# An adaptive-norm attention and feed-forward layer: three late query products instead of two, and their copies behind each step's exponential

## What is computed

```
x = x + attn(cond(x, cond_128, ...), Wq, Wkv, Wo, bo)
x = x + ffn(cond2(x, cond_128, ...), w1, w3, w2, lora...)
attn: q = x@Wq (32 heads of 16), k, v = x@Wkv (8 groups of 16)
      weights = softmax(where(causal, -inf, q k^T) * 0.25);  ctx = weights v;  out = ctx@Wo + bo
ffn:  h1 = lora_linear(x, w1), h3 = lora_linear(x, w3);  lora_linear(silu(h1) * h3, w2)
```

## Time and profile before

| | |
|---|---|
| time, median of 3 runs | 592.26 us (591.83 to 592.91) |
| time of the profiled execution | 592.54 us |
| span of the profiled execution | 590.7 us |
| mean granted clock of PE | 0.991 |
| busy: PE, DVE, ACT, POOL | 578.9, 237.6, 172.2, 182.3 us |
| chain, attention's part | first scores at 101.87 us, first context at 118.30 us; last POOL piece in it at 172.99 us |

### The profile page before, as it was taken

How to read it: one execution, slowest core, us unless ns; L and a number is a source line. 1 busy time by engine, 2 the same in 40 slices (tenths; PEclk the granted TensorE clock), 3 DMA queues, 4 the chain that set the end, 5 groups by cost and what they waited for, 6 DMA issues and landing times.

```text
span 590.7 us, 8111 instructions
## 1 busy us (share of the span) xinstructions
PE 578.9 (98%) x3227; PEld 466.8 (79%) x3227; DVE 237.6 (40%) x340; ACT 172.2 (29%) x296; POOL 182.3 (31%) x132
## 2 busy tenths in 40 slices
PE   9999999799999999999999999999999999999997
PEld 6988988577777778887778888778888777888885
DVE  1434542789999851111641111244111234211112
ACT  3561224564654353332121111121111102211110
POOL 3438463699999595434200000000000000000000
PEclk9999999969999999999999999999999999999999
DMA  7975648545666774000019000007400002200001
GB/s 244 344 306 158 225 161 267 144 102 172 178 157 178 240 220 88 1 0 1 1 71 226 5 1 1 2 1 206 94 0 0 0 0 76 67 0 1 0 1 71
DMA packets 70735, 59.24 MB, mean 100 GB/s; under 512 B 45072, under 2 KB 61840, under 8 KB 69584
## 3 DMA queue, kind: packets, MB, share of 16 engines
q1 hardware_dynamic: 69840, 57.43, 32.2%
q10 hardware_dynamic: 864, 1.38, 0.6%
HBM read 40.94 MB, written 16.79 MB: 98 GB/s over the span
## 4 chain that ended last, share of the span: by engine, by line
PE 84%; POOL 6%; DVE 4%; ACT 2%; SPq 1%; DMA 1%; issue 1%; POOLq 0%; DVEq 0%
PE twin L1333 41%; PE twin L1354 20%; PE twin L1155 7%; POOL probs L646 4%; PE twin L1299 3%; PE twin L1175 3%; PE twin L1188 3%; PE twin L1230 3%; DVE total L997 2%; ACT probs L822 2%; DVE top L980 2%; SPq L463 1%; POOL probs L653 1%; PE twin L1118 1%; DMA down_sb<-in_down_factors 1%; PE twin L1285 1%
## 5 line engine op out<-in xcount | busy, mean ns | idle before, releaser
L1046 DVE TENSOR_TENSOR gate<-twin,gate 128x512 f32<-128x512 f32 (+1 forms) x44 | 30.4, 691 | 244.5 <-PE twin L1333 244.5
L1333 PE MATMUL twin<-c_hi,f_lo 128*128 128x512 f32 (+1 forms) x352 | 96.5, 397 | 0.0
L1333 PE MATMUL twin<-c_hi,f_hi 128*128 128x512 f32 (+1 forms) x352 | 95.4, 393 | 0.0
L1333 PE MATMUL twin<-c_lo,f_hi 128*128 128x512 f32 (+1 forms) x352 | 95.3, 393 | 0.0
L1333 PEld LDWEIGHTS twin<-c_hi,f_lo 128*128 128x128 f32 (+1 forms) x352 | 65.6, 187 | 16.1 <-POOL f_lo L682 0.4
L1333 PEld LDWEIGHTS twin<-c_hi,f_hi 128*128 128x128 f32 (+1 forms) x352 | 65.5, 186 | 15.6 <-issue 0.3
L1333 PEld LDWEIGHTS twin<-c_lo,f_hi 128*128 128x128 f32 (+1 forms) x352 | 65.5, 186 | 15.5
L868 ACT ACTIVATE gate<-twin 128x512 f32<-128x512 f32 (+1 forms) x44 | 26.3, 598 | 169.9 <-PE twin L1333 169.9
L1354 PE MATMUL twin<-f_lo,gate_hi 128*128 128x512 f32 (+1 forms) x176 | 68.6, 390 | 0.0
L871 ACT CAST gate_hi<-gate 128x512 fp32r<-128x512 f32 (+1 forms) x44 | 27.3, 622 | 126.6 <-DVE gate L1046 126.6
L1354 PE MATMUL twin<-f_hi_head,gate_hi 128*128 128x512 f32 x128 | 50.1, 392 | 0.0
(11 more groups left out here) (150 smaller groups left out, 813.8 us busy)
## 6 DMA issues: line engine op xcount, KB each, us to landing
f_sb<-in_f SPq DMA_DIRECT2D x2, 2752.0 KB, 20.1
x_dram<-resid_stage SPq DMA_DIRECT2D x16, 256.0 KB, 2.1
rows<-x_dram SPq DMA_DIRECT2D x16, 256.0 KB, 3.5
q_t<-q_dram SPq DMA_DIRECT2D x8, 512.0 KB, 5.5
x_dram<-rows SPq DMA_DIRECT2D x16, 256.0 KB, 3.3
rows<-x_dram SPq DMA_DIRECT2D x8, 512.0 KB, 4.5
out<-rows SPq DMA_DIRECT2D x12, 256.0 KB, 2.0
x_sb<-in_x SPq DMA_DIRECT2D x2, 1024.0 KB, 7.6
```

The lines of the kernel that those rows point to most:

```text
L1046: dve.tensor_tensor(gate[0:w, h % 2, :], up_bank[2 * (h % 2) + 1][0:w, :], gate[0:w, h % 2, :], ALU.mult).then_inc(gate_ready, 1)
L1333: mm = pe.matmul(bank[0:w, :], f[:, c, :], c_part[:, c, :], start=(n == 0 and c == 0), stop=(n == 2 and c == DC - 1))
```

## The change

`LATE_Q` becomes 3: in the last block q1, q2 and q3 come behind the first scores, q1 and q2 both at step 1 and q3 at step 2 (`LATE_STEPS`). ACT's late copies go from ahead of the exponential to behind it, in the same steps as the projections. All four pieces of `wo_hi` are made ahead of the copy of q0. The four border memsets go from ahead of POOL's loop to its step 5, behind the second multiplication there, together with the wait for `wo_lo`. The packing of the convolution's weights stays at step 2 (`PACK_AT`).

```diff
-LATE_Q = 2
+LATE_Q = 3
+LATE_STEPS = (1, 1, 2)
+PACK_AT = 2
@@ POOL
-            pool.wait_ge(wo_lo_split, REP)
-            for pair in (near_head, near_tail):
-                pool.memset(pair[:, :, :, 0:1], 0.0).then_inc(near_zeroed, 1)
-                pool.memset(pair[:, :, :, WIN - 1:WIN], 0.0).then_inc(near_zeroed, 1)
...
             for n in range(QUADS + OUT):
...
+                if n == SUM + TILES:
+
+                    pool.wait_ge(wo_lo_split, REP)
+                    for pair in (near_head, near_tail):
+                        pool.memset(pair[:, :, :, 0:1], 0.0).then_inc(near_zeroed, 1)
+                        pool.memset(pair[:, :, :, WIN - 1:WIN], 0.0).then_inc(near_zeroed, 1)
@@ ACT, last block of the front
+                    if blk == BLOCKS - 1:
+
+                        act.wait_ge(wo_loaded, 16)
+                        for part in range(REP):
+                            act.copy(wo_hi[:, part, :]...).then_inc(wo_hi_split, 1)
                     for j in range(REP - (LATE_Q if blk == BLOCKS - 1 else 0)):
                         copy_queries(blk, j)
...
-                        if blk == BLOCKS - 1:
-
-                            act.wait_ge(wo_loaded, 16)
-                            for part in range(j * REP // (REP - LATE_Q), (j + 1) * REP // (REP - LATE_Q)):
-                                act.copy(wo_hi[:, part, :]...).then_inc(wo_hi_split, 1)
@@ ACT, attention
-                if 1 <= n <= LATE_Q:
-                    copy_queries(BLOCKS - 1, REP - LATE_Q + n - 1)
...
                     act.activation(probs[:, n % PROBS], probs[:, n % PROBS], ACT.Exp, scale=SCALE)\
                         .then_inc(exp_ready, 1)
-                if n == LATE_Q:
+                for k, step in enumerate(LATE_STEPS):
+                    if n == step:
+                        copy_queries(BLOCKS - 1, REP - LATE_Q + k)
+                if n == PACK_AT:
@@ PE, attention
-                if 1 <= n <= LATE_Q:
-                    project(BLOCKS - 1, REP - LATE_Q + n)
-                if n == LATE_Q:
+                for k, step in enumerate(LATE_STEPS):
+                    if n == step:
+                        project(BLOCKS - 1, REP - LATE_Q + 1 + k)
+                if n == PACK_AT:
                     group_conv()
```

More of the change, by code:

```diff
@@ L770, in _ @@
                                 .then_inc(k_loaded[0], 16)
+                    if blk == BLOCKS - 1:
+                        act.wait_ge(wo_loaded, 16)
+                        for part in range(REP):
+                            act.copy(wo_hi[:, part, :].rearrange("p (h r w) -> p h r w", h=2, r=BT),
+                                     in_windows(wo_sb[:, part, :])).then_inc(wo_hi_split, 1)
                     for j in range(REP - (LATE_Q if blk == BLOCKS - 1 else 0)):
@@ L774, in _ @@
                             copy_up_factors(1 + j)
-                        if blk == BLOCKS - 1:
-                            act.wait_ge(wo_loaded, 16)
-                            for part in range(j * REP // (REP - LATE_Q), (j + 1) * REP // (REP - LATE_Q)):
-                                act.copy(wo_hi[:, part, :].rearrange("p (h r w) -> p h r w", h=2, r=BT),
-                                         in_windows(wo_sb[:, part, :])).then_inc(wo_hi_split, 1)
             copies = stack_copies(a_down, b_down, a_down_s, b_down_s, down_part[2 * S:3 * S, :],
```

## The result

| | before | after |
|---|---|---|
| median | 592.42 us (16 runs, 591.67 to 593.56) | 593.84 us (16 runs, 592.65 to 596.94) |
| ratio, 95% interval | | 1.0027 (1.0016 to 1.0038) |
| profiled execution, its span | 592.54, 590.7 us | 592.98, 591.1 us |
| mean granted clock of PE | 0.991 | 0.996 |

The change costs 1.4 us in the median, and the executions scatter over 4.3 us instead of 1.9 (the kernel before, run more often beside the experiments, scattered over 2.6 and 3.7). The profiled execution is one of the quicker ones, so its trace shows less than the median's loss.

A forecast was written before the change was run, and what follows sets the result against it. PE held 84% of the chain, but near the edit other engines did, POOL alone from 116.87 to 134.73 us. Exponential -0.61 and scores(3) +1.48 made +0.87: 593.4 us, in terms of the median 593.2; range 591.7 to 595.2.

The forecast's parts named there:

- no change: Whole kernel: measured time the same within about 0.2% (1.2 us), chance 0.55, against slower 0.40 and faster 0.05.
- First scores: PE's front with one projection fewer: first scores still wait for the keys' load at 101.87 us; worth nothing.
- Exponential ahead of the copies: ACT, tile 1: exponential starts at 112.75 us instead of 113.36, a gain of 0.61 us.
- Three late projections: PE: q3 waits for ACT's copy of q1, starts at 114.5 us; scores(3) end at 119.7, shift(3) 0.87 us later.
- ACT's other moves: ACT: wo_hi copies ahead of q0's covered by 4.6 us; one more late copy, 0.58 us, fits 1.45 us of idleness.
- POOL's memsets: POOL: removal before the loop gives nothing; at step 5 they cost 0 to 0.28 us, taken as 0.
- The store: SP's queue: store of the last block's queries lands by 126.6 us, ahead of ACT's first output copy, covered by 3 us.
- The clock: PE's granted clock: two new pauses, 3.2 to 3.4 and 2.9 to 3.1 us, were given no cost in the sum.
- the granted clock at 2.4 GHz throughout: Sign of being right on PE; 1.2 GHz between 102 and 120 us would have shown the forecast wrong.
- The two rivals on the clock: PE's clock falls in the pause before q3 (up to 598.3 us) or before the first scores (595.2 us); chance 0.1 each.
- The fall ahead of the first scores: Rival: PE's clock low for 9.2 us, sum(1) at 117.3 us, about +2.9 us, so 595.2 us; chance 0.1.
- The fall ahead of q3: Rival: q3 to scores(3) takes up to twice 5.18 us, shift(3) up to 6.1 us late, up to 598.3 us; chance 0.1.

The follow-up runs named there:

- both pauses filled: Changed kernel with PE kept busy by products nobody reads, 14 ahead of the first scores and 8 behind scores(2): 593.34 us, ratio 1.0015.
- the moves alone: Kernel before with only the four wo_hi copies ahead of the query copies and the four memsets at step 5: 592.30 us, ratio 1.0003.
- the version with q1's copy ahead: Changed kernel with the copy of q1 alone ahead of exponential(1), those of q2 and q3 behind: 592.94 us, ratio 1.0012.
- the first pause filled: Changed kernel with 14 unused products on PE ahead of the first scores alone: 594.89 us, ratio 1.0033.

## Why the prediction was right, and where it wasn't

The median, 593.84, lies in the stated range and near the forecast of 593.2, on the slow side; by 0.27% it is just over the 0.2% that I took as what can be told, so what I held likeliest, no change, was missed and the second, slower, came. That the median lies so near may in part be luck: by the profiles the late scores cost 0.64 us and not 0.87, and the clock, which I had put at nothing, came on top. (The sum itself gives 592.54 + 0.87 - 0.28 = 593.13, so 593.1 and not 593.2.)

*First scores* stay where the load lets them, 101.55: right. *Exponential ahead of the copies*, -0.61 us: right, to 0.01 us by the yardstick, in the version with two late projections (0.4 us between the medians). *Three late projections*: the step of which the forecast is made, right in mechanism and nearly in size. In the profile after, q3 starts 2.94 us behind ACT's first copy of down factors (114.10 - 111.16), where I had 3.12 (114.50 - 111.38): ACT starts the copy of q1 at 113.48, 0.96 us into the exponential and not after 1.08, and the handover to PE took 0.05 us (113.57 + 0.48 to 114.10 in the chain), not 0.1. From q3 to scores(3) 5.17 us against 5.18. So shift(3) was 0.65 us late by the yardstick's origin (122.94 - 111.16 = 11.78 against 122.51 - 111.38 = 11.13) where I had 0.87, and nothing of it was lost or regained up to shift(5) (23.99 - 23.35 = 0.64), as forecast. With both pauses filled it was 0.64 in the profile and 0.9 between the medians. PE took none of q3, packing and scores(3) out of order; the Trainium skill ("TensorE: Matmul & The Clock Gate", Part 2) says that only weight loads overtake, the matmuls stay in program order. The trace agrees: scores(3) started behind the packing products, whose last group began at 117.22, at 117.88.

*ACT's other moves* and *POOL's memsets*: right, nothing, by the moves alone and by shift(6), 5.46 us behind shift(5) as before. *The store*: right as far as the first output copy, which waited for nothing in the profile after.

*The clock* is the step that failed: "By the rows alone both pauses are shorter than what preceded the one fall, so the sum has none." A pause needn't be as long as the one of before: the clock fell at pauses of 3.36, of 3.49 and, in the version with q1's copy ahead, of 2.89 us, twice of these only when PE was at work again. And "the granted clock at 2.4 GHz throughout" was one of my signs of being right. By the rule of the Trainium skill ("TensorE: Matmul & The Clock Gate", Part 1), that the full clock is granted only for recent activity, this could be; the runs show that it is. The two rivals on the clock had a tenth each, and both falls occur. The fall ahead of the first scores was in the profiled execution itself, but cost nearly nothing where I had made it 2.9 us: the low stretch lasted 3.4 us (102.1 to 105.5) and not 9.2, and transposition(2) held sum(1) up by only 0.3 us (113.90 against 112.52 + 1.06 = 113.58, the end of the exponential), which shift(3) did not feel, as scores(3) were later still. The fall ahead of q3 costs up to 6.1 by my bound; 1.5 us of it appear in the profile with the first pause filled (6.68 against 5.17), again because the low stretch is short, 3.4 us.

So the 1.4 us are, by these runs, 0.6 us (profiles) to 0.9 us (medians) of late scores, and the rest in the median, 0.5 to 0.8 us, goes with the clock, which is a tail and not a constant. That the first pause's fall shortens the second pause, and so protects q3, would explain why filling the first alone raised the median to 594.89. The profiles fit (1.42 against 3.49 us of pause), but the intervals of the two ratios overlap, so this is argued and not shown. Which share the third pause, ahead of the second context product, has in the tail wasn't tried; its fall cost about 0.7 us in the profile with q1's copy ahead, and nothing up to shift(5) in the three with pauses filled.

## What to carry to other kernels

Moving a product off a full engine's queue into a gap is only worth something if that queue was what the next stage waited for; here the first scores waited for a load. Where a moved product needs a buffer back, look up who frees it and what stands ahead of that on its engine: two edits that each look free (a product behind the scores, a copy behind the exponential) made a new wait between them. And the better edit was found by reading who the exponential really waited for: a copy whose result nobody needed yet.

## What the runs showed of the hardware

The length of a pause of PE alone didn't decide whether the granted clock fell. It fell at pauses of 1.70 us (two late projections, down copies later), 2.69 (three profiles with pauses filled), 2.89 to 3.49 and 4.02 to 4.49, and did not at one of 2.69 in the changed kernel. The fall came within the pause or up to 1.5 us after PE had resumed. In the changed kernel and with the first pause filled the clock then stayed low for 3.4 us under full work; in the kernel before it stayed low for 10.2 us, of which PE stood still for 2.1. With the first pause alone filled, the same program text took between 592.38 and 596.47 us on one chip; with 8 unused products in the pause ahead of q3 alone it took 592.76 to 593.70, and with none 592.65 to 596.94.
